# Causal mask of an attention block: added by VectorE as it takes the scores from PSUM, in place of two mask products a tile on TensorE

## The reference

```
q, k, v = heads of (x @ Wq.T), (x @ Wk.T), (x @ Wv.T); q, k = layernorm(q), layernorm(k)
scores = einsum("nhld,nhmd->nhlm", q, k)
scores = where(tril(ones(L, L)), scores, NEG)        # the causal mask
attn   = softmax(scores, axis=-1)
out    = einsum("nhlm,nhmd->nhld", attn, v) @ Wo.T + bo
```

## Time and profile before

| | |
|---|---|
| median of 3 runs | 336.92 us (335.68 to 339.65) |
| the profiled execution | 335.12 us, of which the span from first to last instruction is 332.5 us |
| PE busy | 310.0 us, 93% |
| DVE busy | 198.3 us, 60% |
| ACT busy | 171.5 us, 52% |
| POOL busy | 160.0 us, 48% |
| attention (first scores to last select) | 68 to 149 us |

### The profile page before, as it was taken

How to read it: one execution, slowest core, us unless ns; L and a number is a source line. 1 busy time by engine, 2 the same in 40 slices (tenths; PEclk the granted TensorE clock), 3 DMA queues, 4 the chain that set the end, 5 groups by cost and what they waited for, 6 DMA issues and landing times.

```text
span 332.5 us, 6299 instructions
## 1 busy us (share of the span) xinstructions
PE 310.0 (93%) x1926; PEld 263.0 (79%) x1926; DVE 198.3 (60%) x520; ACT 171.5 (52%) x394; POOL 160.0 (48%) x166
## 2 busy tenths in 40 slices
PE   4999999999899999987999889999999999999995
PEld 4987555578788888876788688889998999989873
DVE  0255548889777777898876658858512131221566
ACT  0201544898776667547524495433342455554183
POOL 2001555726887767473000347858774254433261
PEclk9999999999999999999999999999999999999999
DMA  7581611112411111129632356545452356662573
GB/s 237 176 326 40 238 36 58 55 56 86 150 49 46 46 47 47 48 65 442 172 113 62 113 158 191 174 119 169 135 182 95 98 189 192 199 200 80 157 225 95
DMA packets 19959, 44.57 MB, mean 134 GB/s; under 512 B 2292, under 2 KB 12210, under 8 KB 19676
## 3 DMA queue, kind: packets, MB, share of 16 engines
q1 hardware_dynamic: 16380, 36.36, 33.8%
q0 software_dynamic: 2400, 6.56, 6.4%
q10 hardware_dynamic: 1152, 1.32, 1.3%
HBM read 37.01 MB, written 7.22 MB: 133 GB/s over the span
## 4 chain that ended last, share of the span: by engine, by line
PE 74%; DVE 9%; DMA 5%; ACT 4%; issue 3%; POOL 3%; DVEq 0%; SPq 0%; POOLq 0%; ACTq 0%
PE banks L1651 11%; PE banks L1660 10%; PE banks L1569 8%; PE banks L1348 8%; PE banks L1393 6%; PE banks L1466 4%; PE banks L1490 4%; PE banks L1562 3%; PE banks L1398 3%; PE banks L1510 3%; DMA qn_sb<-z_rows,gidx_sb 2%; PE banks L1452 2%; PE banks L1438 2%; DVE h_sb L1336 2%; PE banks L1638 2%
## 5 line engine op out<-in xcount | busy, mean ns | idle before, releaser
L1651 PE MATMUL banks<-qn_sb,w_sb 128*128 128x128 f32 x400 | 49.0, 276 | 1.2 <-ACT qn_sb L717 1.0
L1651 PEld LDWEIGHTS banks<-qn_sb,w_sb 128*128 128x128 f32 x400 | 46.7, 192 | 1.7 <-ACT qn_sb L717 1.2
L1660 PE MATMUL banks<-w_sb,sq_sb 128*128 x200 | 47.1, 379 | 0.0
L525 POOL DMA_INDIRECT y_rows<-pT_sb,sidx_sb x25 | 25.0, 1000 | 41.9 <-DVE pT_sb L1269 41.3
L519 POOL DMA_INDIRECT qn_sb<-z_rows,gidx_sb x25 | 26.7, 1068 | 38.2 <-DVE gidx_sb L1171 22.9
L717 ACT ACTIVATE qn_sb<-banks,col_sb 128x128 f32<-128x128 f32 x50 | 20.2, 455 | 46.6 <-PE banks L1638 45.8
L1660 PEld LDWEIGHTS banks<-w_sb,sq_sb 128*128 128x128 f32 x200 | 36.7, 190 | 4.3
L1269 DVE TENSOR_TENSOR pT_sb<-banks,p_sb 128x256 f32<-128x256 f32 x25 | 10.6, 424 | 48.7 <-PE banks L1660 45.6
L728 ACT ACTIVATE sq_sb<-banks,col_sb 128x128 f32<-128x128 f32 x100 | 31.2, 365 | 12.5 <-PE banks L1651 12.2
L1348 PE MATMUL banks<-patch_sb,wtok_sb 128*128 128x252 f32 (+1 forms) x120 | 26.2, 381 | 4.5 <-DMA wtok_sb<-in_w_tok 4.5
L1348 PEld LDWEIGHTS banks<-patch_sb,wtok_sb 128*128 128x128 f32 x120 | 22.7, 207 | 6.9 <-DMA wtok_sb<-in_w_tok 4.5
(11 more groups left out here) (249 smaller groups left out, 629.8 us busy)
## 6 DMA issues: line engine op xcount, KB each, us to landing
w_sb<-in_w SPq DMA_DIRECT2D x25, 512.0 KB, 3.8
w_sb<-in_w SPq DMA_DIRECT2D x1, 4096.0 KB, 12.3
vrep_sb<-v_rows SPq DMA_DIRECT2D x33, 114.0 KB
patch_sb<-in_patches SPq DMA_DIRECT2D x3, 756.0 KB, 4.3
qk_sb<-y_rows SPq DMA_DIRECT2D x10, 224.0 KB, 4.9
v_rows<-v_sb SPq DMA_DIRECT2D x11, 114.0 KB
z_rows<-h_sb SPq DMA_DIRECT2D x11, 114.0 KB
out_rows<-h_sb SPq DMA_DIRECT2D x10, 112.0 KB
```

The source lines that it names most:

```text
L525: pool.indirect_dma_start(out=y_dram, out_offset=bass.IndirectOffsetOnAxis(ap=sidx_sb[:, j:j + 1], axis=0), in_=ys_sb[:, s * D:(s + 1) * D ...
L1651: last = nc.tensor.matmul(bank[2 + 2 * s + c // 2][:, (c % 2) * 128:(c % 2 + 1) * 128], w1_sb[:, w0:w0 + 128], xsT_sb[:, (2 * s + k) * 128 ...
L1660: last = nc.tensor.matmul(bank[6 + s][:, 0:D], hidT_sb[:, s * HID + k * 128:s * HID + (k + 1) * 128], w2_sb[:, ds(e * 4 * D + k * D, D)], ...
```

## The change

PE's two mask products a tile and the two 16-bit copies go. DVE's `shift` has six operations a tile in place of four: for each half it adds the mask to the bank's scores and writes the sum to p_sb (`masked`), takes the maxima from p_sb (`largest`), and subtracts them in place in p_sb (`shifted`). The order is masked(0), largest(0), masked(1), shifted(0), largest(1), shifted(1). PE now waits for `masked_cr`, which the mask addition raises, before it writes a bank again; ACT's exponential still waits for `shifted_cr`.

```diff
-        idb_sb = sb("idb_sb", T, bf16)
-        maskb_sb = sb("maskb_sb", SEQ, bf16)
...
-            nc.vector.tensor_copy(idb_sb[0:T, :], identT).then_inc(consts_set, 1)
-            nc.vector.tensor_copy(maskb_sb[0:T, :], con_sb[0:T, K_MASK:K_MASK + SEQ]).then_inc(consts_set, 1)
...
             def shift(t, s):
                 if behind(t, 2):
                     dve.wait_ge(p_turned, 2 * t - 2)
-                for hf in range(2):
-                    sc = bank[4 + hf][0:T, 0:CH // 2].rearrange("p (n m) -> p n m", m=SEQ)
-                    mx = mx_sb[0:T, hf * NH // 2:(hf + 1) * NH // 2]
-                    p = p_sb[0:T, s * CH + hf * CH // 2:s * CH + (hf + 1) * CH // 2].rearrange("p (n m) -> p n m", m=SEQ)
+                mask = con_sb[0:T, K_MASK:K_MASK + SEQ].unsqueeze(1).broadcast_to([T, NH // 2, SEQ])
+                mx = [mx_sb[0:T, hf * NH // 2:(hf + 1) * NH // 2] for hf in range(2)]
+                p = [p_sb[0:T, s * CH + hf * CH // 2:s * CH + (hf + 1) * CH // 2].rearrange("p (n m) -> p n m", m=SEQ) for hf in range(2)]
+
+                def masked(hf):
                     dve.wait_ge(scored, 2 * t + hf + 1)
-                    nc.vector.tensor_reduce(mx, sc, AX.X, ALU.max).then_inc(max_set, 1)
+                    nc.vector.tensor_tensor(p[hf], bank[4 + hf][0:T, 0:CH // 2].rearrange("p (n m) -> p n m", m=SEQ), mask,
+                                            ALU.add).then_inc(masked_cr, 1)
+
+                def largest(hf):
+                    dve.wait_ge(masked_cr, 2 * t + hf + 3)
+                    nc.vector.tensor_reduce(mx[hf], p[hf], AX.X, ALU.max).then_inc(max_set, 1)
+
+                def shifted(hf):
                     dve.wait_ge(max_set, 2 * t + hf + 1)
-                    nc.vector.tensor_tensor(p, sc, mx.unsqueeze(2).broadcast_to([T, NH // 2, SEQ]), ALU.subtract).then_inc(shifted_cr, 1)
+                    nc.vector.tensor_tensor(p[hf], p[hf], mx[hf].unsqueeze(2).broadcast_to([T, NH // 2, SEQ]), ALU.subtract).then_inc(shifted_cr, 1)
+
+                masked(0)
+                largest(0)
+                masked(1)
+                shifted(0)
+                largest(1)
+                shifted(1)
...
-            pe.wait_ge(consts_set, 2)
...
                 for hf in range(2):
-                    pe.wait_ge(shifted_cr, 2 * t + hf + 1)
-                    nc.tensor.matmul(bank[4 + hf][0:T, 0:CH // 2], idb_sb[0:T, :], mask8, start=True, stop=False, skip_group_check=True)
+                    pe.wait_ge(masked_cr, 2 * t + hf + 1)
...
-                                                kc_sb[0:96, k0:k0 + 2 * SEQ], start=False, stop=True, skip_group_check=True)
+                                                kc_sb[0:96, k0:k0 + 2 * SEQ], start=True, stop=True, skip_group_check=True)
                     last.then_inc(scored, 1)
```

More of the change, by code:

```diff
@@ L198, in vit_kernel @@
         d_out = sem("d_out")
-        consts_set, half_set = sem("consts_set"), sem("half_set")
+        masked_cr, half_set = sem("masked_cr"), sem("half_set")
         dve_chain, pool_chain = sem("dve_chain"), sem("pool_chain")
@@ L816, in link @@
                 dve.wait_ge(dve_chain, count[0])
-            for s_ in (h_added_cr, v_kept_cr, ss_set_cr, shifted_cr, pre_kept_cr, ys_set_cr):
+            for s_ in (h_added_cr, v_kept_cr, ss_set_cr, shifted_cr, masked_cr, pre_kept_cr, ys_set_cr):
                 dve.sem_inc(s_, 2)
@@ L1453, in turn_k @@
                 last.then_inc(k_turned, 1)
-            mask8 = maskb_sb[0:T, :].unsqueeze(1).broadcast_to([T, NH // 2, SEQ])
             def scores(t, s):
```

## The result

The changed kernel took 350.21 us (median of 4 runs, 348.88 to 352.43), the kernel before 337.84 us (4 runs, 335.68 to 339.65). The ratio is 1.040, with a 95% interval of 1.035 to 1.046: 12.4 us slower by the medians, 11.7 to 15.5 by the interval. Forecast were 352 us and a range of 342 to 357.

What follows compares the result with a forecast made beforehand. A PE-ACT loop set the tile; after the change DVE and POOL, excluding each other, would. Start 3.8, six tiles 9.2 and end 2.5 sum to 15.5 us on 336.9: 352 us, range 342 to 357.

Steps and rivals of the forecast that it cites:

- What bounds the kernel: Steady attention tile: a PE-ACT loop sets 7.58 us; removing mask products gains 0 there, up to 2.8 us if uncovered.
- The cost of the operations: DVE's shift without collisions: additions and SBUF reductions 0.47 us each, six operations +0.79 us a tile, within DVE's waits.
- The exclusion: Steady tiles: DVE's subtractions with two SBUF inputs and POOL's operations wait for each other; tile 9.1 us, +1.5.
- start, to select(1): First tiles of attention: subtractions of shift(0) and shift(1) meet POOL's operations; select(1) ends 3.8 us late.
- six tiles: POOL's steps 2 to 7: the collision costs +1.5 us in each tile, 9.2 us in all.
- end, to the mark: Last attention steps, measured to the start of ACT's 2.54 us copy: +2.5 us, after some comes back.
- rival 1: Steady tiles: first subtraction slips in before POOL's kn; half to none of 9.2 us lost, 343 to 348, chance 0.22.
- step 8: Near attention's end, POOL has less to do: no wait needed, 7.0 us in place of 7.5.
- step 9: Near attention's end: the second subtraction falls on POOL's power operation of 2.60 us, +3.5 us.
- The clock: Granted clock while PE's waits grow from 0.6 to about 2.5 us a tile: no cost taken, small chance of one.
- Rival 2: DVE's subtraction: its small second operand does not exclude POOL, so no collision; 334 to 337 us, chance 0.12.
- Rival 3: Attention stage: POOL's queue always served first, or clock at its lower level in part; 357 to 370 us, chance 0.09.

Runs made afterwards that it cites:

- e6: Kernel before without its mask products and without any causal mask; median 337.8 us, ratio 1.003 to the kernel before.
- e7: Kernel before with one more of the six pieces of k moved from ACT to DVE; median 338.4 us, ratio 1.003 to the kernel before.
- e1: Changed kernel with the maxima written to spare PSUM bank columns, PE waiting for the subtraction; median 339.4 us, ratio 1.005 to the kernel before.
- e3: Changed kernel with DVE's six operations ordered half by half; median 345.4 us, ratio 1.026 to the kernel before.
- e4: Changed kernel with TensorE's two mask products a tile put back, so the mask is added twice; median 351.5 us.
- e5: Changed kernel with two unused matmuls a tile filling PE's wait ahead of turn_k from tile 3; median 349.5 us, ratio 1.040 to the kernel before.

## Why the prediction was right

**What bounds the kernel: held.** e6 shows that TensorE's products were hidden. e7 shows that ACT's pieces of k are in the loop: one piece less gave 0.33 us a tile of its 0.6 (keep_k 1.09 us in place of 1.70). What is next is then DVE's keep_k, which the view names as the releaser of the output product:

```profile
104.51 1.09 PE L1509 MATMUL banks<-wo_sb,attT_sb 128*114 128x256 f32 x4 [0.27 <-DVE kc_sb L941]
```

**The cost of the operations: held.** Additions 0.470, reductions from SBUF 0.468 against 0.47 each. The errata section of the Trainium skill's "VectorE: DVE Perf Modes" would have made the SBUF reduction 0.06 us shorter than one from PSUM; here they are 0.468 and 0.472 in the median, so the measurement decides for the row.

**The exclusion: held, and shown by e1.** Against select's end at 108.86 the tile reads: first subtraction due at +3.06 (forecast 3.07), ended at +4.84 (4.86), second ended at +6.50 (6.56), select at +8.93 (9.1). Of the 0.17 us that are missing, 0.06 lie in the subtractions; the rest lies in finish and select, which overlap what stands before them by 0.06 us each when DVE comes to them without a wait; I had added the lengths of before. POOL's vd was stretched by 0.22 us, not by 0.3 to 0.4. That the one input decides is the rule of the Trainium skill's "SBUF — State Buffer", section "Who interferes with whom": two SBUF inputs contend, one does not. The prediction also took from it that the hold lasts the whole instruction; for one of POOL's operations that did not come true, see below.

**The sum, term by term.** At each mark, time after minus time before:

| term | forecast | measured |
|---|---|---|
| start, to select(1) | +3.8 | 91.06 - 87.29 = +3.8 |
| six tiles | +9.2 | 53.4 - 45.2 = +8.2 |
| end, to the mark | +2.5 | 17.1 - 16.0 = +1.1 |
| at the mark | +15.5 | +13.0 |
| whole run, medians | +15.5 | +12.4 |

The start was right by luck in its last half microsecond. Select(0) ended 3.3 us late, as worked out. But the first subtraction of shift(2) was due 0.03 us before kn and slipped in (86.47, 0.47 us), which is rival 1 in one tile; L1009 then waited for the delayed spread and took 1.17 us in place of 0.21, which made up for it.

**The term that was mis-sized: the end.** Of its three parts, step 8 came to -0.8 (forecast -0.5), step 9 to +1.4 (+3.5), and what follows to +0.5 (-0.5). I priced the second subtraction of shift(10) as waiting for POOL's power operation of 2.60 us. DVE and POOL there, in the changed kernel:

```profile
152.77 1.47 POOL L460 TENSOR_TENSOR vd_sb<-vrep_sb,con_sb 114x768 f32<-114x768 f32 x1
...
153.41 1.17 DVE L986 TENSOR_TENSOR p_sb<-p_sb,mx_sb 114x304 f32<-114x304 f32 x1
154.20 2.83 POOL L499 TENSOR_TENSOR rr_sb<-rr_sb,half_sb 114x14 f32<-114x14 f32 x1
...
154.99 0.47 DVE L986 TENSOR_TENSOR p_sb<-p_sb,mx_sb 114x304 f32<-114x304 f32 x1
```

The second subtraction ran in 0.47 us in the middle of the power operation, and it did so in e3, e4 and e5 too. POOL's operation was held at its start, by 0.23 us (2.83 against 2.60), while the first subtraction was still at work; after that it held nobody. Without that stall step 9 took 6.6 us and not the forecast 8.7 (5.2 of before and 3.5). Part of the saving was lost because PE ran at the lower clock there: its values product took 2.58 us at 158.34 in place of 1.75. At a full clock nothing of the +1.1 is left: e4 and e5 take 15.8 us for this stretch, the kernel before 16.0.

The trace of before had the sign. There L998, with two SBUF inputs, ran inside the power operation and took its 0.21 us:

```profile
143.67 2.60 POOL L501 TENSOR_TENSOR rr_sb<-rr_sb,half_sb 114x14 f32<-114x14 f32 x1
143.94 0.21 DVE L998 TENSOR_TENSOR rci_sb<-rc_sb,con_sb 114x48 f32<-114x48 f32 x1
```

I had read one instance of L998 as held, at 0.416 us, and had not looked where the other ten stood.

**The clock: the assumption was off.** I took no cost and gave a small chance to a fall. The clock did fall, to 0.966 in the profiled execution, and a granted clock below full stood among the signs of being wrong. In the steady tiles it cost nothing, at the end of the stage 1.3 us, and behind the mark, where the prediction had nothing change, this execution is 5.1 us longer than that of before. Between the medians nothing of the 5.1 is left, since the kernel before had its lower clocks too: its median span is 335.3 us, 2.8 above that of its profiled execution, and 348.4 is 13.1 more, against 13.0 at the mark. The 0.8 us less outside the span make the rest of the way to +12.4.

PE's waits, which were to be 2 us a tile, were 1.8 in the tile that ends at 108.86, none in the next, in which PE ran slow, and 0.9 in the one after.

**Rival 2** (a small second operand does not collide) falls with the 1.25 us of the subtraction. **Rival 3** falls in its first half (POOL always first) with e3, where DVE takes its turn between two POOL operations that stand back to back. Its second half came true as a condition, the clock was at its lower level in part of the stage, but not with its price of 357 to 370.

## What to carry to other kernels

Before moving elementwise work to DVE, count how many of its tensor inputs lie in SBUF, and look at what POOL runs at that moment: here an operand of 8 numbers a row, moved from SBUF to spare columns of the PSUM bank, was worth 13 us. Work taken from the busiest engine is worth only what that engine does not wait for: PE was busy 93% of the span, and the products taken from it were worth nothing. Where two engines exclude each other, the order of a few operations decides who waits; try the order as well as the amount.

## What the runs showed of the hardware that was not expected

- The exclusion did not last as long as POOL's power operation on 114x14 numbers, which runs 2.6 us: a subtraction with two SBUF inputs ran in it at 0.47 us, 0.8 us after its start (changed kernel), and L998 at 0.21 us, 0.27 us after its start (kernel before). For POOL's operations on 114x672 and 114x768 numbers the wait lasted to their end. Whether it is the few numbers or the kind of operation that makes the difference, no run shows.
- The exclusion has a joint: whichever side waits ends about 0.13 us sooner after the other's end than its duration alone would say. Subtractions that waited ended 0.33 us after POOL's operation (113.37 to 113.70), 0.47 alone; POOL's spread ended 1.33 us after the subtraction (113.70 to 115.03), 1.48 alone.
- The mean granted clock of the unchanged kernel varied between 0.985 and 1.000 from execution to execution, and the time with it, 340.6 to 334.5 us. Differences below 1% need many runs, or a mark inside the profile.
